# Four graph layers on one core: the LSTM and the first part of layer 2 in one Block

## What is computed

```python
x = _layernorm(x + _L0_gnn_ref(x, adj, ...))   # spectral, over eigenvectors of the Laplacian
x = _layernorm(x + _L1_gnn_ref(x, adj, ...))   # two mixing products, then four LSTM passes
x = _layernorm(x + _L2_gnn_ref(x, adj, ...))   # A_hat, 256 -> 512, batch norm, relu, 512 -> 256, batch norm
x = _layernorm(x + _L3_gnn_ref(x, adj, adj, ...))  # masked attention and a sum over children
```

```python
for p in range(1, MAX_SKIP + 1):
    wins = h[:, :nw * p, :].reshape(Bv * nw, p, Hd)
    last = _lstm_last(Wih[p - 1], Whh[p - 1], bih[p - 1], bhh[p - 1], wins)
    h = h.at[:, idx, :].set(last.reshape(Bv, nw, Hd))
```

## Time and profile before

| | before |
|---|---|
| median of three runs | 2201.55 us |
| the profiled execution | 2200.56 us |
| its span | 2198.8 us |
| TensorE busy | 1820.8 us (83%) |
| VectorE / ScalarE / GpSimd busy | 1462.6 / 868.5 / 648.8 us |
| last matmul of the LSTM ends | 1690.47 us |
| first transpose of layer 2's first part | 1697.97 us |
| last operation of that part (VectorE, L2375) | 1853.5 us |

### The profile page before, as it was taken

The page is one execution under the profiler, slowest core; times in us unless marked ns, Lnnn a source line. Parts: engine busy times, 40 slices in busy tenths (PEclk is TensorE's granted clock), DMA queues, the critical chain, the costliest instruction groups (busy, mean ns, idle before and its releaser), DMA issues. The chain is left out here.

```text
span 2198.8 us, 31909 instructions
## 1 busy us (share of the span) xinstructions
PE 1820.8 (83%) x9508; PEld 1535.3 (70%) x9508; DVE 1462.6 (67%) x5810; ACT 868.5 (39%) x1784; POOL 648.8 (30%) x1034
## 2 busy tenths in 40 slices
PE   3454433326999899999999999999998898979997
PEld 2333333305998688888899999888886787856664
DVE  7999999985777456445534444443444677868886
ACT  2333222201443466333333333332332565746664
POOL 0010344402322466333323332422240112521111
PEclk9999766657999999999999999999999899989998
DMA  6000000000100100000000000000000411210111
GB/s 187 2 1 1 1 1 1 1 1 20 49 39 39 39 16 18 10 10 10 7 8 10 10 10 0 1 1 0 17 2 31 180 63 65 96 39 30 39 39 48
DMA packets 44683, 62.63 MB, mean 28 GB/s; under 512 B 13968, under 2 KB 33296, under 8 KB 44432
## 3 DMA queue, kind: packets, MB, share of 16 engines
q1 hardware_dynamic: 43968, 61.08, 8.2%
q10 hardware_dynamic: 592, 0.17, 0.0%
HBM read 36.08 MB, written 25.17 MB: 28 GB/s over the span
## 5 line engine op out<-in xcount | busy, mean ns | idle before, releaser
L2023 ACT ACTIVATE l_gates<-ps,biases 128x512 f32<-128x512 f32 (+1 forms) x504 | 288.9, 635 | 501.4 <-remote 486.3
L1957 PE MATMUL ps<-l_nodes_in,l_even 128*128 128x512 f32 x1392 | 319.2, 389 | 0.5 <-remote 0.4
L1957 PE MATMUL ps<-l_nodes_in,kept 128*128 128x336 f32 (+1 forms) x1280 | 299.6, 351 | 9.1 <-remote 7.3
L1957 PEld LDWEIGHTS ps<-l_nodes_in,l_even 128*128 128x128 f32 x1392 | 261.1, 188 | 55.4 <-issue 1.3
L2068 DVE TENSOR_TENSOR l_gates<-l_gates 128x512 f32<-128x512 f32 (+1 forms) x72 | 49.8, 692 | 342.4 <-ACT l_gates L2023 342.4
L1912 POOL CAST l_nodes_in<-big 128x512 fp32r (+3 forms) x142 | 100.6, 737 | 546.7 <-remote 531.7
L1957 PEld LDWEIGHTS ps<-l_nodes_in,kept 128*128 128x128 f32 x1280 | 230.4, 189 | 35.0 <-issue 11.7
L1957 PE MATMUL ps<-l_state,l_even 128*128 128x512 f32 x960 | 220.8, 389 | 0.0
L1957 PEld LDWEIGHTS ps<-l_state,l_even 128*128 128x128 f32 x960 | 180.2, 188 | 37.4
L1915 POOL TENSOR_TENSOR l_nodes_in<-big,l_nodes_in 128x512 fp32r<-128x512 f32 (+1 forms) x142 | 200.9, 1435 | 5.7
L994 PE MATMUL ps<-w,sw_xT 128*128 128x128 f32 x256 | 60.2, 429 | 124.3 <-ACT sw_xT L858 124.3
(11 more groups left out here) (561 smaller groups left out, 3929.6 us busy)
## 6 DMA issues: line engine op xcount, KB each, us to landing
x<-in_x SPq DMA_DIRECT2D x4, 2048.0 KB, 16.9
residual<-s_x SPq DMA_DIRECT2D x16, 512.0 KB, 2.6
x_late<-residual SPq DMA_DIRECT2D x16, 512.0 KB, 10.9
normed<-j_x SPq DMA_DIRECT2D x16, 512.0 KB, 2.6
x_late<-normed SPq DMA_DIRECT2D x16, 512.0 KB, 3.2
out<-a_y SPq DMA_DIRECT2D x16, 512.0 KB, 2.9
l_raw<-in_L_gnn_W SPq DMA_DIRECT2D x16, 256.0 KB, 2.8
l_raw<-in_L_gnn_W SPq DMA_DIRECT2D x4, 512.0 KB, 3.6
```

The costliest lines, as they stand in the source:

```text
L1957: return pe.matmul(ps[:, 4 * j + gate, 0:n], w[w_part][:, at:at + 128].bitcast(F32R), src[:, part, k, 0:n].bitcast(F32R), start=start, sto ...
L2023: act.activation(gates[:, j, gate, 0:n], ps[:, 4 * j + gate, 0:n], ACT.Tanh if gate == G else ACT.Sigmoid, bias=bias[:, gate * KD + j:gate ...
```

## The change

Both Blocks become one function with one Block, `lstm_and_widen`. Its parts:

- **Space.** `x` now lies where `odd`, `nodes_in` and `even` lie: they are 16384 numbers per partition together. Groups 0 to 3 share with `odd` (free once pass 3 is over), 4 to 7 with `nodes_in` and 8 to 15 with `even` (both in use until the LSTM's last matmul). `x2` lies in `raw`, and the high and low parts of the aggregation in `state`. The buffer `r` goes: the sum is written over x.
- **The last round of pass 4** is written out behind a loop of three rounds. In its steps 2 and 3 the groups 0 and 1 are transposed into banks 6 and 7 (gates G and O of half 1) between the products of half 0 and half 1, added, measured and normalised. The order of the gates there is I, FG, then G and O after the wait for the addition.
- **The last step** is interleaved with the first steps of layer 2. ScalarE makes the high part of group 0 between the gates of halves 0 and 1, VectorE ends the new state of half 0 after the norm of group 2 and that of half 1 before the norm of group 3. TensorE goes on with `aggregate(0)`, then `turn`, `widen`, `aggregate`, `widen` as before from g = 2. `turn(12)` waits for these states, as groups 12 to 15 hold the last round's tokens.
- **The wide weights** are loaded when pass 4 begins and split by GpSimd before its last round, not after it.
- **Loads and stores.** Groups 0 to 3 of x are loaded when GpSimd gets to the last round, groups 4 to 15 after `aggregate(0)`. The stores of groups 0 and 1 come before the latter, those of 2 to 15 after them.
- **Waits.** The addition doesn't wait for the former group's normalisation; GpSimd's power waits for it instead, and VectorE's minus_mean waits for the former group's power.

The diff, cut to its core:

```diff
 class CountedNorm:
-    def __init__(self, nc, ctx, name):
+    def __init__(self, nc, ctx, name, sums=None):
...
+    def r(self, g):
+        return self.sums(g) if self.sums else self.shared
...
     def power(self, pool, g):
         pool.wait_ge(self.var_ready, g + 1)
+        if g and self.sums:
+            pool.wait_ge(self.written, TILES * g)
...
     def add(self, dve, g, psum, residual):
-        if g:
+        if g and not self.sums:
             dve.wait_ge(self.written, TILES * g)
...
-            sp.wait_ge(raw_free, 1)
+            sp.wait_ge(last_pass, 1)
             for source, at, _ in wide:
...
+            sp.wait_ge(odd_free, 1)
+            for g in range(4):
+                sp.dma_start(tiles_of(g), residual[g]).then_inc(x_landed[g], 16)
...
+            for g in range(EARLY):
+                store(g)
+            sp.wait_ge(a_ready, 1)
+            for g in range(4, GROUPS):
+                sp.dma_start(tiles_of(g), residual[g]).then_inc(x_landed[g], 16)
+            for g in range(EARLY, GROUPS):
+                store(g)
...
         @block.tensor
+                def one_step(i, g=-1):
+                    step, slot = i % p, i % 2
+                    order = (I, G, O) if step == 0 else (I, G, FG, O)
...
+                    for j in range(KD):
+                        pe.wait_ge(banks_free[j], 1)
+                        pe.sem_clear(banks_free[j])
+                        if j and g >= 0:
+                            turn(g)
+                            of_nodes(j, step, nodes_in[:, slot], (I, FG))
+                            pe.wait_ge(ln.added, g + 1)
+                            mm = of_nodes(j, step, nodes_in[:, slot], (G, O))
+                        else:
+                            mm = of_nodes(j, step, nodes_in[:, slot], order)
...
+                with pe.Fori(0, rounds - (p == SKIPS)):
                     for i in range(span * p):
+                        one_step(i)
+            for i in range(SKIPS):
+                one_step(i, early_group(i))
...
+            pe.wait_ge(banks_free[0], 1)
+            aggregate(0)
+            for g in range(EARLY, GROUPS + 2):
+                if g < GROUPS:
+                    turn(g)
+                widen(g - 2, (0, 1))
+                if g <= GROUPS:
+                    aggregate(g - 1)
+                widen(g - 2, (2, 3))
...
         @block.scalar
+            act.wait_ge(wide_ready, 1)
+            for i in range(SKIPS - 1):
+                if early_group(i) >= 0:
+                    norm(early_group(i))
+                one_step(i)
+            norm(EARLY - 1)
+            inputs(0)
+            rest(0, SKIPS - 1)
+            inputs(1)
+            high(0)
+            rest(1, SKIPS - 1)
+            squash(0)
+            for g in range(EARLY, GROUPS + 2):
...
+                if g == EARLY:
+                    squash(1)
...
         @block.vector
+            for i in range(SKIPS - 1):
+                if early_group(i) >= 0:
+                    norm(early_group(i))
+                one_step(i, LAST)
+            norm(EARLY - 1)
+            add_input(SKIPS - 1, 0)
+            forget(SKIPS - 1, 0)
+            add_input(SKIPS - 1, 1)
+            low(0)
+            for g in range(EARLY, GROUPS + 2):
+                if g < GROUPS:
+                    norm(g)
+                if g == EARLY:
+                    new_state(LAST, SKIPS - 1, 0).then_inc(layer1_ready, 1)
+                    forget(SKIPS - 1, 1)
+                measure(g - 2, (0, 1))
+                if g <= GROUPS:
+                    low(g - 1)
+                measure(g - 2, (2, 3))
+                if g == EARLY:
+                    new_state(LAST, SKIPS - 1, 1).then_inc(layer1_ready, 1)
...
         @block.gpsimd
+                if cut.p == SKIPS:
+                    pool.sem_inc(odd_free, 1)
...
+                    pool.wait_ge(wide_landed, 16 * len(wide))
...
+                    pool.sem_inc(wide_ready, 1)
                 split_round(cut, cut.rounds - 1, last=True)
```

More of the change, by code:

```diff
@@ L1558, in statistics @@
         for i in range(TILES):
-            dve.bn_stats(self.stats[:, i, :], self.r[:, i, :]).then_inc(self.measured, 1)
+            dve.bn_stats(self.stats[:, i, :], self.r(g)[:, i, :]).then_inc(self.measured, 1)
         dve.wait_ge(self.measured, done + TILES)
@@ L1563, in statistics @@
         dve.wait_ge(self.measured, done + 2 * TILES)
+        if g and self.sums:
+            dve.wait_ge(self.rstd_ready, g)
         dve.tensor_scalar(self.minus_mean[:, :, :], self.mean[:, :, 0:1], -1.0, None, ALU.mult)
@@ L2819, in bass_four_graph_layers_kernel @@
         kept = sb("kept", [128, 4096])
-        early = ctx.enter_context(ExitStack())
-        x = sb("x", [128, TOKENS // TILE, WIDTH], early)
+        with ExitStack() as place:
+            x = sb("x", [128, TOKENS // TILE, WIDTH], place)
+        odd, nodes_in = sb("l_odd", [128, 4096]), sb("l_nodes_in", [128, 2, 2, KD, GROUP])
+        even = [sb(f"l_even{part}", [128, 4096]) for part in range(2)]
         rest_loaded, w0_loaded = ctx.semaphore("rest_loaded"), ctx.semaphore("w0_loaded")
@@ L2904, in bass_four_graph_layers_kernel @@
                                     (W["L1_gnn_W"][0][:, 0:half_kept], kept[:, 0:half_kept], kept[:, half_kept:]), biases2)
-        early.close()
         wide = {"w1": kept[:, 0:2048].rearrange("p (a n) -> p a n", a=2),
                 "w2": kept[:, 2048:4096].rearrange("p (a n) -> p a n", a=2)}
-        with Stage(nc) as third:
-            lstm(nc, third, ps, big, [W["L1_gnn_W"][p] for p in range(SKIPS)], biases2[:, 0, :, :], kept[:, :],
-                 ((by_rows("L2_gnn_W1T"), 0, wide["w1"]), (by_rows("L2_gnn_W2T"), 1024, wide["w2"])))
-        x = sb("x_late", [128, TOKENS // TILE, WIDTH])
-        w3 = {"wq": sb("wq", [128, KD, HEAD]), "wk": sb("wk", [128, KD, HEAD]), "wv": sb("wv", [128, KD, HEAD]),
-              "wo": sb("wo", [128, WIDTH]), "bo": sb("bo", [128, WIDTH]), "bq": c["bq"], "bk": c["bk"], "bv": c["bv"]}
         w3_loaded = ctx.semaphore("w3_loaded")
+        w3 = {"bq": c["bq"], "bk": c["bk"], "bv": c["bv"]}
         def load_attention(sp):
@@ L2922, in load_attention @@
             sp.dma_start(w3["bo"][:, :], W["L3_gnn_bo"].partition_broadcast(128)).then_inc(w3_loaded, 16)
-        with Stage(nc) as fourth:
-            stats1, stats2 = sb("stats1", [128, FC2, GROUPS, 6], fourth), sb("stats2", [128, KD, GROUPS, 6], fourth)
-            bn1 = BatchNorm(nc, fourth, "bn1", stats1, FC2, c["b2_1"], c["g2_1"], c["be2_1"], c["scale1"], c["offset1"])
-            bn2 = BatchNorm(nc, fourth, "bn2", stats2, KD, c["b2_2"], c["g2_2"], c["be2_2"], c["scale2"], c["offset2"])
+        with Stage(nc) as third:
+            stats1, stats2 = sb("stats1", [128, FC2, GROUPS, 6], third), sb("stats2", [128, KD, GROUPS, 6], third)
+            bn1 = BatchNorm(nc, third, "bn1", stats1, FC2, c["b2_1"], c["g2_1"], c["be2_1"], c["scale1"], c["offset1"])
+            bn2 = BatchNorm(nc, third, "bn2", stats2, KD, c["b2_2"], c["g2_2"], c["be2_2"], c["scale2"], c["offset2"])
             with Stage(nc) as inner:
-                join_and_widen(nc, inner, t, ps, m, wide, x, residual, normed, big, stats1, bn1)
-            normalised_products(nc, fourth, ps, wide, x, normed, big, c["scale1"], c["offset1"], stats2, bn2,
-                                load_attention, lambda sp: sp.wait_ge(w3_loaded, 5 * 16))
-        with Stage(nc) as fifth:
-            attention(nc, fifth, t, ps, m, w3, x, big, c["scale2"], c["offset2"], out)
+                lstm_and_widen(nc, inner, t, ps, m, big, x, [W["L1_gnn_W"][p] for p in range(SKIPS)],
+                               biases2[:, 0, :, :], kept[:, :], odd, nodes_in, even, wide,
+                               ((by_rows("L2_gnn_W1T"), 0, wide["w1"]), (by_rows("L2_gnn_W2T"), 1024, wide["w2"])),
+                               residual, normed, stats1, bn1)
+            w3 |= {name: sb(name, [128, KD, HEAD], third) for name in ("wq", "wk", "wv")}
+            w3 |= {name: sb(name, [128, WIDTH], third) for name in ("wo", "bo")}
+            with Stage(nc) as fourth:
+                normalised_products(nc, fourth, ps, wide, x, normed, big, c["scale1"], c["offset1"], stats2, bn2,
+                                    load_attention, lambda sp: sp.wait_ge(w3_loaded, 5 * 16))
+            with Stage(nc) as fifth:
+                attention(nc, fifth, t, ps, m, w3, x, big, c["scale2"], c["offset2"], out)
 _TURNED = {"L2_gnn_W1": "L2_gnn_W1T", "L2_gnn_W2": "L2_gnn_W2T"}
```

752 lines of the change are left out of this document (360 added, 392 removed).

## The result

| | before | after |
|---|---|---|
| median | 2201.66 us (4 runs) | 2188.73 us (4 runs, 2187.96 to 2189.54) |
| the profiled execution | 2200.56 us | 2187.96 us |
| its span | 2198.8 us | 2186.2 us |
| last matmul of the LSTM ends (E) | 1690.47 us | 1701.42 us |
| addition of group 5 | 1745.38 us | 1733.32 us |

The ratio is 0.9941, with a 95% interval of 0.9924 to 0.9958: 12.9 us faster.

What follows compares the result with a forecast made beforehand. The prediction saw a TensorE-bound LSTM round, a hole and a slow start of layer 2. Gaining 22.5 us there and paying 4.1 in the early steps gave -18.4: 2201.55 to 2183.2 us, range 2178.5 to 2189.5.

Steps and rivals of the forecast that it cites:

- The hole: Between the LSTM's last matmul and layer 2: TensorE idle, 7.4 us together with the Blocks' meeting, to be removed.
- the barrier: Both Blocks meet after the LSTM; counted within the 7.4 us in which TensorE does nothing.
- the load of x: Start of layer 2: group 0 waits for x, 3.4 us before, hidden by loading earlier.
- the two groups in series: Start of layer 2: first two groups run one after the other, 14.0 us before the change.
- the stall by the store: Start of layer 2: group 0's store behind sixteen loads held ScalarE 4.6 us, within an 11.9 us step; to go.
- part 5: Start of layer 2: addition of group 5 at E + 32.4, not 54.9; gain 22.5 us, bounds 21 to 25.
- the half clock: Start of layer 2: TensorE began at half clock after 7.43 us without a matmul; 1.00 throughout was expected.
- part 1: Two groups inside the LSTM's last round, steps 2 and 3: cost 4.1 us together, bounds 2.1 to 8.5.
- part 2: x placed where odd weights, nodes and even weights were: loads hidden, ScalarE's 4.6 us store stall goes.
- early waits of 3.2 us: Rival, steps 2 and 3: TensorE waits up to 3.2 us, not 1.0, twice; +4.4, 2187.6 us; chance 0.08.
- part 4: Join in layer 2, in place instead of buffer r: period stays at 8.61 us, worth nothing.
- part 3: Wide weights split a round earlier, before the last round: its small loss moves and stays, worth nothing.

Runs made afterwards that it cites:

- both mended: The changed kernel with state in step with the weights and the first 8 products with the state before the early waits: 2181.88 us, ratio 0.9905.

## Why the prediction was right, and where it was off

- **The hole, the barrier, the load of x, the two groups in series, the stall by the store** (part 5): 22.5 forecast, 23.0 found, and each addition 0.3 to 0.6 us before its forecast. The stall was shown by itself (2.7 us by the medians, 4.3 in the profile); what the hole, the load and the half clock are worth one by one was not separated.
- **The early steps** (part 1): 4.1 forecast, 4.7 found (the last round without early groups, in the same layout, is 73.97 us, with them 78.64). The waits were 0.97 and 1.34, forecast 1.0 each. In step 3 VectorE stood still for 0.5 us between two of its own operations, which I had not seen in the rows and don't explain.
- **The term that was mis-sized is part 2**, the move of x onto `odd`, `nodes_in` and `even`. I cost it as transfers alone and so at nothing. It puts `state` 64 bytes out of step with the weights (modulo 256), and every product with it in passes 2 and 4 takes 2.5 ns more. The kernel with the tensors in step measures 4.5 us less (3.4 by its windows), and its 2184.25 is 1.1 from the forecast. The range held the time all the same, but by luck: its upper end was made of early waits of 3.2 us, which did not come, and the term that nobody had reckoned with took their place.
- **In place** (part 4): right for the steady flow, where the period is 8.61 us in both; wrong as a general nothing, since at the start the second addition comes 3.7 us sooner behind the first where groups stand close. In the change itself nothing stands on it, because the early groups are a step apart.
- **The wide split** (part 3) moved with its loss, as forecast, but the loss grew: before, the last round was 0.4 us longer than its neighbours (73.85 to 73.44, from start to start), now the third is 0.6 longer (74.60 to 73.96).
- **The clock** stayed at 1.00 in the last round. The rule of the Trainium skill ("TensorE: Matmul & The Clock Gate", Part 4: PE-mode transpose) that transposes don't count as TensorE's activity for its clock did not decide here: 8 transposes and a wait of 1.34 us amid dense matmuls left the clock at 1.00. The margin was smaller than the hole of 7.43 us suggests: in the kernel before, 8 transposes and a wait of 2.92 us were followed by half clock, and the longer early wait of 3.2 us among the rivals would have been no shorter than that.
- **Not of the change**: the matmuls ahead of pass 1 ran at a clock of 0.63 in the profiled execution after and at 1.00 in that before, so 12 of them took 4.58 and 2.99 us. Among the variants both occur, though this part of the program is the same in all. Pass 1 itself took 133.77 us in the kernel with state in step and 132.58 in the one with both mended, whose tensors lie alike. So 2.6 of the 10.95 us by which E is later are, as far as these profiles tell, chance of two single executions. The rest is 1.4 in passes 2 and 3, 2.1 in the first three rounds of pass 4 and 4.8 in the last.

```profile
729.24:733.82 4.58, 4.58 (x12) 3.29 (x12) 0.75 (x1) 0.00 (x0) 0.00 (x0) 0.63 0.00 0
```

```profile
729.38:732.37 2.99, 2.99 (x12) 2.15 (x12) 0.75 (x1) 0.00 (x0) 0.00 (x0) 1.00 0.00 0
```

What stays open: whether the period of 256 bytes holds for other widths and types, why pass 3 with its 336 columns slows with some shifts and not with others, and why 64 costs 2.5 ns, and 128 and 192 cost 6.7 ns a matmul.

## What to carry to other kernels

Work that would fill a pipeline's start can be put into the last steps of the loop ahead; reckon its price from the engine that must answer inside the step, and give the waiting engine products that need nothing new. When tensors are moved in SBUF, write down the distance modulo 256 bytes between each matmul's moving operand and its weights before and after: it is a term of the sum where TensorE is the bound (shown here for float32r products of 512 columns). A store queued behind a long row of loads holds the buffer that it frees; load only as far ahead as is needed.

## What the runs showed of the hardware

- Float32r matmuls of 128 x 512, each with a new weight load, come every 226.7 ns when the moving operand lies a multiple of 256 bytes from the weights, every 229.2 ns at 64 and every 233.3 ns at 128 and 192 bytes (10.88, 11.00 and 11.20 us for 48). The Trainium skill ("SBUF — State Buffer", on its two separate sides) says that among the engines only the port pair shared by VectorE and GpSimd causes contention and that TensorE never waits for anyone. That is about one engine waiting for another, and these runs show something else: the other engines' work is the same (in the first round of pass 4 VectorE is busy 29.91 us after and 29.86 before), and yet TensorE's matmuls lengthen with the place of its own two operands.
- In pass 3, with 336 columns, a shift of 64 bytes between `kept` and both moving operands changed nothing (passes 2 and 3: 523.94 us to 523.95). With 128 bytes between `kept` and the nodes, and 64 either way between `state` and its weights, it took 286.5 us in place of 284.5.
